# Fourteen unread products ahead of one transposition, and other turning points for three engine loops

## The chip, the cores and the metric

The kernel runs on one core of a Trainium2 chip. The metric is the time of one launch in microseconds, as the device counts it; three runs of the kernel before gave a median of 2035.68 us (2034.31 to 2038.46). The core has five engines that run their own instruction lists and meet only at semaphores: PE (TensorE, products and transpositions), DVE (VectorE), ACT (ScalarE), POOL (GpSimd) and SP (SyncE, which here issues the transfers of x and of the result).

## The reference, cut to what matters

Input x is 32 graphs of 512 nodes with 128 features, adj is one 512 x 512 matrix of zeros and ones that all graphs share. Four layers follow, each `x = layernorm(x + layer(x))`:

```python
x = _layernorm(x + _L0_gnn_ref(x, adj, q, k, v))      # attention, masked with adj
x = _layernorm(x + _L1_gnn_ref(x, adj, Wi, ..., bm))  # gated edges, two small networks
x = _layernorm(x + _L2_gnn_ref(x, adj, weight, bias)) # Chebyshev filter: adj products twice
x = _layernorm(x + _L3_gnn_ref(x, adj, adj, ..., 5))  # five steps of a gated recurrent unit
```

In layer 3 each step computes `m = adj @ h`, gates `r` and `z` from `m` and `h`, a candidate `tanh(...)`, and the new `h`. All is fp32; the large products are taken as two or three passes of high and low parts.

## The kernel before, in words

The 32 graphs are worked on in 8 rounds (0 to 7) of 4 slots (0 to 3); a graph lives in its slot's buffers for a whole round. A round is cut into stages with names: x0, query, scores, mix for layer 0; x1, xh, gates, edges, agg, self, out1 for layer 1; x2, cheb01, cheb23, lap1, lap2 for layer 2; x3 and then m, uh, r, v, rh, t with a step number 0 to 4 for layer 3. "m4.3" is stage m4 of slot 3. `spread` and `norm` 0 to 3 are the layer norms: DVE takes statistics, POOL computes the scale (L396 to L401), ACT applies it (L471).

The order in which an engine takes its stages is fixed ahead of time. `body(engine)` (L119) lays the 64 stages of the 4 slots on one period, shifted per slot and per engine by the numbers in SCHEDULE, and sorts them; what has run past the end of the period is put at its start and marked `behind`, which means that it works for the round before. `run` (L137) writes the stages out three times per engine: the stages of round 0 that are not behind as straight code, then a loop `Fori(1, ROUNDS)` over the whole list, then the stages that are behind once more:

```python
run("tensor", stages, 0, first=True)
with pe.Fori(1, ROUNDS) as r:
    run("tensor", stages, r)
run("tensor", stages, ROUNDS, last=True)
```

So each loop makes seven passes and jumps back six times; the step from the straight code into the loop and the step out of it are no jumps back. Where the list begins is where the loop turns. Before, the turn of all four loops lies at the same part of a round, its end:

- PE: ... m4.3, v4.2, t4.1, uh4.3, rh4.2, r4.3, turn, x0.0, v4.3, t4.2, ...
- ACT: ... m4.2, v4.1, rh4.1, r4.2, turn, m4.3, v4.2, rh4.2, ...
- DVE: ... m4.2, r4.1, last.0, rh4.1, turn, m4.3, r4.2, spread3.0, last.1, rh4.2, ...
- POOL: ... v4.0, m4.2, turn, v4.1, ...

Lines that the rows name: L881 is the transposition helper of PE (x0, x1, x2, x3 and t; `ident` with xin is x0, with X is x1, x2 or x3); L886 to L888 are the three passes of a split product (with U_hi stage uh, with Gw_hi stages r and v, with C_hi stage cheb); L1022 and L1023 are lap1 and lap2; L1050 and L1051 are the eight products of a stage m; L1080 is rh. On DVE L679 writes a low part (gT_lo in stage m), L836 is stage r, L841 and L845 are the two halves of stage rh. On ACT L465 copies a transposition to xT_hi, L471 is a norm, L558 and L559 copy x3's transposition, L563 belongs to stage m. On POOL L425 writes xT_lo in stage m, L430 is stage v.

Around layer 3's start PE's order is lap2.1, lap2.3, x3.0, m0.0, x3.1, uh0.0, m0.1, x3.2, uh0.1, r0.0, m0.2, x3.3, uh0.2, ...; x3.0 waits until ACT has written slot 0's third norm. Before that PE's order around layer 2's start is out1.3, x2.0, x2.1, cheb01.0, x2.2, cheb01.1, x2.3, ...

Of the kernel before, what the change touches and what calls it, by code (L numbers as in the profile page):

```python
# [29 lines left out]
P = 128  # L30
# [83 lines left out]
def elag(engine, n):  # L114

    return SCHEDULE[n][LAGS[engine]] if engine in LAGS else 0.0


def body(engine):  # L119


    period = sum(length for _, length in STAGES) + SLOT_LAG
    at = []
    for s in range(SLOTS):
        time = (s // 2) * PAIR_LAG + (s % 2) * SLOT_LAG
        for n, (name, length) in enumerate(STAGES):
            if name == "lap1" and s % 2 == 0 or name == "spread2" and s % 2 == 1:
                time += SLOT_LAG
            if name not in ("lap1", "lap_lo", "lap2") or s % 2:
                t = time + elag(engine, n)  # L130
                at.append((t % period, s, n, name, int(t // period)))
            time += length
    assert all(behind in (0, 1) for *_, behind in at)
    return [(name, s, behind) for _, s, _, name, behind in sorted(at)]


def run(engine, stages, r, first=False, last=False):  # L137

    for name, s, behind in body(engine):
        if name in stages and not (first and behind) and not (last and not behind):  # L140
            stages[name](s, r - behind)
# [20 lines left out]
TURNS, XTS, GTS, NHS, COPIES, PRODUCTS, VECTORS, POOLS = map(len, (TURNED, XT, GT, NH, COPIED, PRODUCT, VECTOR, POOL))  # L162
DS = 129
NORMS = 4


def build(nc, x, adj, q, k, v, Wi, bi, We, be, Wn, bn, Wm, bm, cheb_w, cheb_b,
# [7 lines left out]
    with ExitStack() as ctx:  # L175
        def sb(name, shape, dt=F32):
            return ctx.enter_context(nc.sbuf_tensor(name, shape, dt))
# [15 lines left out]
        adjT_hi = sb("adjT_hi", [P, TILES, N], F32R)  # L193
# [54 lines left out]
        psA = [ctx.enter_context(nc.psum_tensor(f"psA{s}", [P, N], F32)) for s in range(SLOTS)]  # L248
        psB = [ctx.enter_context(nc.psum_tensor(f"psB{s}", [P, N], F32)) for s in range(SLOTS)]
# [87 lines left out]
        def _(sp):  # L337
# [14 lines left out]
            for r in range(ROUNDS):  # L352
                for s in range(SLOTS):
                    if r + 1 < ROUNDS:
                        sp.wait_ge(residual[s], NORMS * r + 2)
                        sp.dma_start(xin[s][:, :, :], xg[(r + 1) * SLOTS + s]).then_inc(loaded[s], 16)
                for s in range(SLOTS):
                    sp.wait_ge(normed[s], NORMS * (r + 1))
                    sp.dma_start(og[r * SLOTS + s], X[s]).then_inc(stored[s], 16)
# [4 lines left out]
        def _(pool):  # L364
# [28 lines left out]
            def norm(s, r, layer):  # L393

                pool.wait_ge(var_ready[s], NORMS * r + layer + 1)
                nc.gpsimd.tensor_tensor(neg_mean[s][:, :], zero_cols[:, :], mv[s][:, :, 0], ALU.subtract).then_inc(pool_done[s], 1)  # L396
                nc.gpsimd.tensor_tensor(rstd[s][:, :], mv[s][:, :, 1], eps_cols[:, :], ALU.add).then_inc(pool_done[s], 1)
                pool.wait_ge(pool_done[s], POOLS * r + POOL[f"var{layer}"])
                nc.gpsimd.tensor_tensor(rstd[s][:, :], rstd[s][:, :], neg_half[:, :], ALU.pow).then_inc(pool_done[s], 1)  # L399
                pool.wait_ge(pool_done[s], POOLS * r + POOL[f"rstd{layer}"])  # L400
                nc.gpsimd.tensor_tensor(shift[s][:, :], neg_mean[s][:, :], rstd[s][:, :], ALU.mult).then_inc(pool_done[s], 1)  # L401

            def stage_x1(s, r):

                pool.wait_ge(normed[s], NORMS * r + 1)
                pool.wait_ge(turned[s], TURNS * r + TURNED["x1"])
# [20 lines left out]
            def stage_v(s, r, k):  # L427
# [5 lines left out]
                      "cheb23": stage_cheb23}  # L433
            for n in range(NORMS):
                stages[f"spread{n}"] = lambda s, r, n=n: norm(s, r, n)
# [9 lines left out]
        def _(act):  # L445
# [107 lines left out]
            def stage_x3(s, r):  # L553
                i, o = s // 2, s % 2
                act.wait_ge(normed[s], NORMS * r + 3)
                nc.scalar.copy(nh_hi[i][:, :, o, :], X[s]).then_inc(nh_hi_ready[s], 1)
# [320 lines left out]
        def _(pe):  # L877
            def transpose_tiles(dst, src):

                for t in range(TILES):  # L880
                    last = nc.tensor.transpose(dst[:, t * P:(t + 1) * P], src(t), ident[:, :])  # L881
                return last
# [29 lines left out]
            pe.wait_ge(s_flag, 1)  # L912
            inexact = pe.value_load(flag[0:1, 0:1])

            def stage_x0(s, r):
                pe.wait_ge(loaded[s], 16 * r + 16)
                pe.wait_ge(residual[s], NORMS * r + 1)
                transpose_tiles(psA[s], lambda t: xin[s][:, t, :]).then_inc(turned[s], 1)
# [117 lines left out]
                lap(s // 2, psB, exact)  # L1036

            def stage_x3(s, r):
                pe.wait_ge(normed[s], NORMS * r + 3)
                transpose_tiles(psA[s], lambda t: X[s][:, t, :]).then_inc(turned[s], 1)  # L1040

# [44 lines left out]
            def rounds(exact):  # L1086

                stages = {"x0": stage_x0, "query": stage_query, "scores01": stage_scores01, "scores23": stage_scores23,
                          "mix": stage_mix, "x1": stage_x1, "xh": stage_xh, "gates": stage_gates,
                          "edges": stage_edges, "agg": stage_agg, "sums1": stage_sums1, "self": stage_self, "out1": stage_out1, "x2": stage_x2,  # L1090
                          "cheb01": stage_cheb01, "cheb23": stage_cheb23,
                          "lap1": lambda s, r: stage_lap1(s, r, exact), "lap2": lambda s, r: stage_lap2(s, r, exact), "x3": stage_x3}
                for k in range(STEPS):
                    stages[f"m{k}"] = lambda s, r, k=k: stage_m(s, r, k, exact)
                    stages[f"uh{k}"] = lambda s, r, k=k: stage_uh(s, r, k)
                    stages[f"r{k}"] = lambda s, r, k=k: stage_r(s, r, k)
                    stages[f"rh{k}"] = lambda s, r, k=k: stage_rh(s, r, k)
                    stages[f"v{k}"] = lambda s, r, k=k: stage_v(s, r, k)
                    stages[f"t{k}"] = lambda s, r, k=k: stage_t(s, r, k)
# [4 lines that stand above are left out]
# [31 lines left out]
```

## Time and profile before

| what | value |
|---|---|
| median of three runs | 2035.68 us (2034.31 to 2038.46) |
| the profiled execution's own time | 2039.13 us |
| its span, first to last instruction | 2036.8 us |
| mean granted TensorE clock | 0.962 of 2.4 GHz |
| busy: PE, DVE, ACT, POOL | 1856.7, 1472.1, 1354.7, 921.1 us |
| on the chain that ended last: PE, DVE, issue, POOL, ACT | 65%, 13%, 8%, 7%, 7% |

The profile is of one execution. A row of windows gives the stretch in us, its length, the busy time and the instructions of PE, PE's weight loads, DVE, ACT and POOL, and then the granted clock (PEclk, 1.00 is 2.4 GHz), the share of the transfer engines and what they moved in GB/s; a stretch runs from the first product of the one named stage to that of the other. A row of a timeline gives start, duration, engine, line, operation, what is written and read, and in brackets the engine's idle time just before it and what ended it. "issue" is idle time in which the engine waited for nothing that the profile shows.

### The profile page before, as it was taken

Reading aid. Unit: us, or ns where it says so; the run is one execution under the profiler, and the core shown is the slowest. Engines: PE = TensorE matmul, PEld = TensorE weight load, DVE = VectorE, ACT = ScalarE, POOL = GpSimd, SP = SyncE. Lnnn points to the kernel's source line nnn. Section 1 sums busy time; section 2 is a strip of 40 time slices with the busy share of each in tenths; the row PEclk is TensorE's granted clock in tenths of the full one; section 3 lists DMA queues with packets and bytes.
Section 4 is the critical chain, followed back from the end, with each engine's and each line's share of the span. In section 5 each row is a group of like instructions: output and inputs, shape, how many; then the busy total and the mean of one; then the engine's idle time right before and its main releaser. Section 6 shows DMA issues by size and latency. Waiting matters only on the chain.

```text
span 2036.8 us, 27531 instructions
## 1 busy us (share of the span) xinstructions
PE 1856.7 (91%) x9307; PEld 1442.9 (71%) x9307; DVE 1472.1 (72%) x3054; ACT 1354.7 (67%) x2689; POOL 921.1 (45%) x1009
## 2 busy tenths in 40 slices
PE   3899998899998999889998899989999889989997
PEld 2776776777767777577775777757768677676775
DVE  6786688766687667866778667786667866678666
ACT  0766677576766767566775667756768666686666
POOL 2354445445364442634436344363444544345344
PEclk6999999999999999999999999999999999999998
DMA  2000001000010000100000000100001000000000
GB/s 69 22 1 0 1 1 42 1 1 1 7 37 1 1 1 12 32 1 0 1 24 21 1 1 1 43 1 1 1 2 42 0 1 1 2 22 1 0 1 22
DMA packets 13514, 21.32 MB, mean 10 GB/s; under 512 B 2720, under 2 KB 5024, under 8 KB 13216
## 3 DMA queue, kind: packets, MB, share of 16 engines
q1 hardware_dynamic: 10768, 18.68, 2.7%
q8 instruction: 87, 1.43, 0.3%
q10 hardware_dynamic: 2576, 0.53, 0.1%
q14 instruction: 83, 0.68, 0.1%
HBM read 10.82 MB, written 8.39 MB: 9 GB/s over the span
## 4 chain that ended last, share of the span: by engine, by line
PE 65%; DVE 13%; issue 8%; POOL 7%; ACT 7%; DMA 0%; DVEq 0%; SPq 0%; POOLq 0%; ACTq 0%
PE psA L1080 7%; PE psA L1050 7%; PE psA L1051 7%; PE psA L881 5%; PE psB L886 5%; PE psB L888 5%; PE psB L887 5%; PE psA L886 3%; PE psA L888 3%; PE psA L887 3%; PE psB L949 3%; PE psA L949 3%; DVE E L753 2%; ACT X L471 2%; PE psB L1074 2%
## 5 line engine op out<-in xcount | busy, mean ns | idle before, releaser
L430 POOL TENSOR_TENSOR S<-S,H 128x512 f32<-128x512 f32 x160 | 225.1, 1407 | 486.3 <-ACT S L573 486.3
L1050 PE MATMUL psA<-adjT_hi,nh_hi 128*128 128x512 f32 x640 | 275.0, 430 | 11.9 <-ACT H L559 11.6
L471 ACT ACTIVATE X<-X,shift,rstd 128x128 f32<-128x128 f32 x512 | 210.4, 501 | 90.2 <-POOL shift L401 89.2
L1051 PE MATMUL psA<-adjT_hi,nh_lo 128*128 128x512 f32 x640 | 259.8, 406 | 0.0
L425 POOL TENSOR_TENSOR xT_lo<-H,xT_hi 128x512 fp32r<-128x512 f32 x160 | 219.2, 1383 | 71.0 <-ACT xT_hi L581 38.1
L841 DVE SCALAR_TENSOR_TENSOR E<-E 128x512 f32<-128x512 f32 x160 | 181.7, 1135 | 63.3 <-ACT E L577 60.4
L836 DVE SCALAR_TENSOR_TENSOR E<-E,H 128x512 f32<-128x512 f32 x160 | 128.5, 803 | 115.1 <-ACT E L567 114.7
L679 DVE TENSOR_TENSOR gT_lo<-psA,gT_hi 128x512 fp32r<-128x512 f32 x160 | 108.8, 688 | 115.0 <-ACT gT_hi L563 101.1
L396 POOL TENSOR_TENSOR neg_mean<-zero_cols,mv 128x4 f32<-128x4 f32 x128 | 30.8, 240 | 356.1 <-DVE mv L696 355.8
L1080 PE MATMUL psA<-E,u5T 128*128 128x512 f32 x320 | 165.0, 597 | 13.7 <-DVE E L836 13.7
L571 ACT ACTIVATE E<-psB,z_bias 128x512 f32<-128x512 f32 x160 | 110.4, 690 | 81.3 <-PE psB L1074 79.8
L1050 PEld LDWEIGHTS psA<-adjT_hi,nh_hi 128*128 128x128 f32 x640 | 124.5, 195 | 52.1 <-issue 10.8
L567 ACT ACTIVATE E<-psB,r_bias 128x512 f32<-128x512 f32 x160 | 110.1, 688 | 61.7 <-PE psB L888 61.1
L845 DVE SCALAR_TENSOR_TENSOR H<-E,S 128x512 f32<-128x512 f32 x160 | 142.2, 889 | 9.3
L563 ACT CAST gT_hi<-psA 128x512 fp32r<-128x512 f32 x160 | 92.6, 591 | 81.4 <-PE psA L1051 80.8
L1051 PEld LDWEIGHTS psA<-adjT_hi,nh_lo 128*128 128x128 f32 x640 | 125.0, 195 | 29.4 <-issue 3.8
L399 POOL TENSOR_TENSOR rstd<-rstd,neg_half 128x4 f32<-128x4 f32 x128 | 136.4, 1066 | 10.0
L577 ACT ACTIVATE E<-psA,hv_bias 128x512 f32<-128x512 f32 x160 | 109.6, 685 | 26.9 <-PE psA L1080 24.7
L753 DVE SCALAR_TENSOR_TENSOR E<-E,edge_mask 128x512 f32<-128x512 f32 x128 | 124.9, 1034 | 0.0
L976 PE MATMUL psA<-E,U 128*128 128x512 f32 x256 | 115.7, 594 | 0.0
L689 DVE BATCH_NORM_STATS2 stat<-X 128x6 f32<-128x128 f32 x512 | 110.6, 278 | 1.4
L516 ACT ACTIVATE E<-psB,src_bias 128x512 f32<-128x512 f32 x128 | 77.6, 688 | 49.1 <-DVE src_bias L746 24.8
(224 smaller groups left out, 5317.1 us busy)
## 6 DMA issues: line engine op xcount, KB each, us to landing
xin<-in_x SPq DMA_DIRECT2D x32, 256.0 KB, 3.0
out<-X SPq DMA_DIRECT2D x32, 256.0 KB, 2.0
E<-in_adj SPq DMA_DIRECT2D x1, 1024.0 KB, 5.7
E<-in_L_gnn_w_w SPq DMA_DIRECT2D x3, 128.0 KB, 7.2
E<-in_L_gnn_weight SPq DMA_DIRECT2D x1, 192.0 KB, 6.8
E<-in_L_gnn_u_w SPq DMA_DIRECT2D x2, 64.0 KB, 6.9
Wm_sb<-in_L_gnn_Wm ACTq DMA_DIRECT2D x1, 128.0 KB, 7.0
E<-in_L_gnn_q SPq DMA_DIRECT2D x1, 64.0 KB, 5.5
```

Source lines behind the costliest of these rows:

```text
L425: nc.gpsimd.tensor_tensor(xT_lo[s][:, :], H[s][:, :], xT_hi[s][:, :].bitcast(F32), ALU.subtract).then_inc(pool_done[s], 1)
L430: nc.gpsimd.tensor_tensor(kept[s], kept[s], H[s][:, :], ALU.mult).then_inc(pool_done[s], 1)
L471: last = nc.scalar.activation(X[s][:, t, :], X[s][:, t, :], ACT.Identity, scale=rstd[s][:, t:t + 1], bias=shift[s][:, t:t + 1])
L753: nc.vector.scalar_tensor_tensor(out=E[s][:, t, :], in0=E[s][:, t, :], scalar=1.0, in1=edge_mask[:, t, :], op0=ALU.add, op1=ALU.mult).then ...
L841: nc.vector.scalar_tensor_tensor(out=h_new[s], in0=z_gate[s], scalar=1.0, in1=h_new[s], op0=ALU.add, op1=ALU.mult).then_inc(vector_done[s], 1)
L845: nc.vector.scalar_tensor_tensor(out=H[s][:, :], in0=h_new[s], scalar=0.5, in1=kept[s], op0=ALU.mult, op1=ALU.add).then_inc(vector_done[s], 1)
L886: nc.tensor.matmul(dst, w_hi, m_hi, start=start, stop=False)
L887: nc.tensor.matmul(dst, w_hi, m_lo, start=False, stop=False)
L888: return nc.tensor.matmul(dst, w_lo, m_hi, start=False, stop=stop)
L1050: nc.tensor.matmul(psA[s][:, :], hi, adjT_hi[:, m, :], start=(m == 0), stop=False)
L1051: last = nc.tensor.matmul(psA[s][:, :], lo, adjT_hi[:, m, :], start=False, stop=(exact and m == TILES - 1))
L1080: nc.tensor.matmul(psA[s][:, :], U5[:, :], rh[s], start=False, stop=True).then_inc(product[s], 1)
```

## The change

Two edits, both in the order of the work. First, `body` rotates the list of three engines, so that their loops turn at another stage: PE's between x2.1 and cheb01.0, ACT's between lap1.3 and norm2.0, DVE's between m2.3 and r2.0. All stages keep their order on their engine; only which copy of the code a stage comes from changes, and where the jump back lies. POOL's list and SP's are left as they are. Second, PE gets 14 products of 128 x 512 (a tile of the adjacency matrix with a row of it) at the head of stage x3 of slot 0, ahead of that stage's wait. They write psA of slot 0, which the transpositions behind the wait overwrite; nothing reads them. No wait and no transfer is added or taken away.

```diff
+TURN_AT = {"tensor": ("cheb01", 0), "scalar": ("norm2", 0), "vector": ("r2", 0)}
 def body(engine):
...
-    return [(name, s, behind) for _, s, _, name, behind in sorted(at)]
+    order = [(name, s, behind) for _, s, _, name, behind in sorted(at)]
+    if engine in TURN_AT:
+        k = [(name, s) for name, s, _ in order].index(TURN_AT[engine])
+        assert not any(behind for *_, behind in order[k:])
+        order = [(name, s, 1) for name, s, _ in order[k:]] + order[:k]
+    return order
...
+WARM = {"x3": [(0, 0, 0, 14)]}
...
+            def keep_warm(name, s):
+
+                for slot, bank, owner, count in WARM.get(name, ()):
+                    if slot == s:
+                        for _ in range(count):
+                            nc.tensor.matmul((psA, psB)[bank][owner][:, :], adjT_hi[:, 0, 0:P], adjT_hi[:, 0, :],
+                                             start=True, stop=True)
...
             def stage_x3(s, r):
+                keep_warm("x3", s)
                 pe.wait_ge(normed[s], NORMS * r + 3)
                 transpose_tiles(psA[s], lambda t: X[s][:, t, :]).then_inc(turned[s], 1)
```

## Rows read from the trace of the kernel before

**Rows 1.** The page's first part: busy time, share of span, instructions of each engine.

```profile
PE 1856.7 (91%) x9307; PEld 1442.9 (71%) x9307; DVE 1472.1 (72%) x3054; ACT 1354.7 (67%) x2689; POOL 921.1 (45%) x1009
```

**Rows 2.** The waits of PE: idle time in total, times, longest.

```profile
PE psA L881 <- issue: 10.2, 6, 2.3
```

**Rows 3.** Windows (PEclk third last): m4.3 to x2.0, round 0; rounds 1-6 summed.

```profile
277.14:370.43 93.29, 85.74 (x476) 64.89 (x475) 77.74 (x195) 65.56 (x133) 47.24 (x60) 1.00 0.07 24
...
sum 596.19, PE 535.23 PEld 404.83 DVE 471.81 ACT 393.96 POOL 285.75; mean PE 89.21 PEld 67.47 DVE 78.64 ACT 65.66 POOL 47.62
```

**Rows 4.** Timeline of the turn from round 1 to round 2, all engines.

```profile
521.67 0.69 DVE L845 SCALAR_TENSOR_TENSOR H<-E,S 128x512 f32<-128x512 f32 x1
522.44 0.59 ACT L563 CAST gT_hi<-psA 128x512 fp32r<-128x512 f32 x1 [1.93 <-PE psA L1051]
...
524.50 1.27 POOL L430 TENSOR_TENSOR S<-S,H 128x512 f32<-128x512 f32 x1 [3.41 <-ACT S L573]
524.86 0.69 DVE L679 TENSOR_TENSOR gT_lo<-psA,gT_hi 128x512 fp32r<-128x512 f32 x1 [2.50 <-issue]
...
526.37 1.13 PE L1080 MATMUL psA<-E,u5T 128*128 128x512 f32 x2 [2.20 <-DVE E L836]
...
530.07 1.11 PE L881 MATMUL psA<-ident,xin 128*128 128x128 f32 x4 [1.60 <-issue]
```

**Rows 5.** Windows: rh4.2 to the next query.0; round 0, round 1.

```profile
281.54:288.18 6.64, 6.10 (x29) 4.13 (x28) 5.84 (x21) 4.51 (x8) 2.88 (x4) 1.00 0.00 0
526.37:536.47 10.10, 8.50 (x29) 5.93 (x29) 6.42 (x23) 4.21 (x7) 1.27 (x2) 0.66 0.02 4
```

**Rows 6.** Timeline of round 2 around the start of cheb01.0.

```profile
619.53 0.42 PEld L881 LDWEIGHTS psA<-ident,X 128*128 128x128 f32 x4 [0.22 <-ACT X L471]
...
621.90 0.45 PE L886 MATMUL psA<-C_hi,xT_hi 128*128 128x384 f32 x1 [1.71 <-DVE xT_lo L679]
...
623.06 0.60 PE L881 MATMUL psA<-ident,X 128*128 128x128 f32 x4
...
624.66 0.56 ACT L465 CAST xT_hi<-psA 128x512 fp32r<-128x512 f32 x1
```

**Rows 7.** Windows: x2.0 to lap1.1; round 2, then rounds 1 to 6 summed.

```profile
618.95:632.78 13.83, 11.38 (x67) 10.09 (x65) 8.71 (x27) 12.85 (x41) 4.64 (x10) 1.00 0.00 1
...
sum 83.92, PE 70.39 PEld 63.34 DVE 52.24 ACT 77.17 POOL 27.84; mean PE 11.73 PEld 10.56 DVE 8.71 ACT 12.86 POOL 4.64
```

**Rows 8.** Timeline of round 1 around x3.0 and m0.0.

```profile
399.75 0.28 PE L1023 MATMUL psB<-nh_lo,adjT_hi 128*128 128x256 f32 x1
...
401.65 1.65 ACT L471 ACTIVATE X<-X,shift,rstd 128x128 f32<-128x128 f32 x4 [7.41 <-POOL shift L401]
...
403.35 0.66 PE L881 MATMUL psA<-ident,X 128*128 128x128 f32 x4 [3.32 <-ACT X L471]
...
405.77 0.63 PE L1051 MATMUL psA<-adjT_hi,nh_lo 128*128 128x512 f32 x1
...
407.90 0.57 PE L1050 MATMUL psA<-adjT_hi,nh_hi 128*128 128x512 f32 x1
...
409.46 0.50 PE L886 MATMUL psB<-xT_hi,U_hi 128*128 128x512 f32 x1 [0.31 <-POOL xT_lo L425]
...
410.71 0.39 PE L1051 MATMUL psA<-adjT_hi,nh_lo 128*128 128x512 f32 x1
...
412.11 0.39 PE L1051 MATMUL psA<-adjT_hi,nh_lo 128*128 128x512 f32 x1
```

**Rows 9.** Windows: x3.0 to rh0.0; round 1, then all eight rounds summed.

```profile
403.35:423.43 20.08, 18.60 (x78) 14.21 (x79) 10.36 (x29) 15.56 (x32) 8.64 (x13) 0.92 0.00 1
...
sum 165.78, PE 151.76 PEld 115.97 DVE 87.54 ACT 124.45 POOL 67.52; mean PE 18.97 PEld 14.50 DVE 10.94 ACT 15.56 POOL 8.44
```

**Rows 10.** Timeline of round 1 around DVE's stage r2.0.

```profile
465.28 0.69 DVE L679 TENSOR_TENSOR gT_lo<-psA,gT_hi 128x512 fp32r<-128x512 f32 x1 [1.18 <-ACT gT_hi L563]
...
468.89 2.80 DVE L836 SCALAR_TENSOR_TENSOR E<-E,H 128x512 f32<-128x512 f32 x4 [2.92 <-ACT E L567]
```

## The prediction

> **What bounds the kernel now.** I read the page first: PE is busy for 91% of the span [rows 1], so an edit pays where PE stands still or runs at 1.2 GHz, and nowhere else. PE's waits say where: six times it stood before a transposition with nothing to wait for [rows 2]. Six is the number of jumps back that each loop makes in seven passes. The timeline of one such place shows the loops turning one after another: DVE restarts at 524.86, 3.19 us after its last instruction before the jump began at 521.67; PE gets its rh4.2 only then, at 526.37, after 2.20 us idle; and then PE itself turns and restarts with x0.0 at 530.07 [rows 4]. The windows give the price. The stretch from m4.3 to the next round's x2.0 takes 93.29 us from round 0 to round 1, where the code runs straight into the loop, and 596.19 / 6 = 99.37 us in the six rounds with a jump [rows 3]. The stages are the same, so a turn costs 6.08 us. Part of it is the clock: behind the turn PE ran at 0.66 of 2.4 GHz, against 1.00 without a jump [rows 5].
>
> The second weak place is the start of layer 3. PE's last product of lap2.3 starts at 399.75, x3.0's transpositions at 403.35, when ACT's norm has ended [rows 8]. After that pause the products of m0.0 start (407.90 - 405.77) / 5 = 0.426 us apart, those of m0.1 (412.11 - 410.71) / 6 = 0.233 us [rows 8]: 1.2 and 2.4 GHz.
>
> **The change part by part.** The sum is made against the profiled execution, 2039.13 us (span 2036.8); the median of the runs, 2035.68, is 3.45 lower, and the result is moved by as much.
>
> *The turns leave the end of the round.* PE, ACT and DVE then run from m4.3 to x2.0 in each round as they did from round 0 to 1. POOL still turns there, and round 0 does not show that; but in a jump round the 3.41 us in which POOL stood before L430 were ended by ACT, not by its own sequencer [rows 4], so its turn was over by then. What is late next is the dependence of rh4 and t4 among themselves, which round 0's 93.29 contains. Gain: 596.19 - 6 x 93.29 = 36.5 us. Bounds: 0 if something else in those rounds made them longer, 36.5 in full.
>
> *ACT's turn* goes ahead of norm2.0, where ACT is idle for 7.41 us [rows 8]. At the old place ACT was idle for 1.93 us over its turn [rows 4]. Cost 0; if that cover went, up to 1.93 a round, on the chain to x3.0.
>
> *DVE's turn* goes between m2.3's L679, started at 465.28, and r2.0's L836 at 468.89: 3.61 us from start to start [rows 10], where the old turn needed 3.19 [rows 4]. Cost 0, with 0.4 us to spare; without cover at most 3.19 a round.
>
> *PE's turn* goes between x2.1 and cheb01.0. Queued behind it is all of cheb. At the old place PE took 3.70 us from the start of rh4.2, after which only six products ran, to its restart [rows 4]; the mean pause before the restart is 10.2 / 6 = 1.70, not the 1.60 of this row [rows 2], so 3.80. At the new place the last released work starts at 619.53 and cheb01.0 at 621.90, 2.37 later [rows 6]. So cheb01.0 comes 1.43 us late. Some of that is hidden: ACT takes the transposition of x2.2 only at 624.66 [rows 6], being busy for 12.85 of the 13.83 us of this stretch [rows 7]. With the restart at 623.33, six products (621.90 to 623.06) and x2.2 (0.60) end at 625.09, 0.43 late. If the clock falls to 1.2 GHz in the longer pause, these 1.76 us become 1.76 x 0.426 / 0.233 = 3.22 and end 1.89 late. The clock does fall here already in some rounds, with the shorter pause: the sum of 83.92 is 0.94 more than six times round 2's 13.83, which had a clock of 1.00 [rows 7]. I take 1.3 a round, two thirds at the slow clock, part of the way: 6 x 13.83 + 7.8 - 83.92 = +6.9 us. Bounds a round: 0, if the sequencer jumps while products are still queued, and 10.10 - 6.64 = 3.46, all that PE's own turn and its clock cost at the old place [rows 5]; as a sum -0.9 to +19.8.
>
> *The 14 products* do the work of 14 x 0.233 = 3.26 us at 2.4 GHz. They are released at once, behind the product of 399.75, and x3.0 comes 3.60 us after that one's start [rows 8]: they fit, with 0.34 less that one product to spare. Nothing waits for them but the four transpositions. They cost nothing as long as the clock is at 2.4 GHz when they start, as it is through lap2; at 1.2 GHz they would take 14 x 0.426 = 5.96 and make x3.0 2.4 us late.
>
> *What a warm start of layer 3 is worth* is less than it seems. In round 1 m0.0 would end 8 x 0.193 = 1.5 us earlier, but uh0.0 waits for POOL's xT_lo [rows 8], and POOL hangs on norms that PE's clock doesn't touch. Only ACT's copies behind x3.1 come earlier; I take 0.2 us. But round 1, with 20.08 us at a clock of 0.92, is a good one: the eight took 165.78, 20.72 in the mean [rows 9], so others lost more, where already the transpositions ran slowly. With every round at 20.08 - 0.2 = 19.9, the eight take 159.2 instead of 165.78: -6.6 us. Bounds: 0, if POOL holds everything, and 8 x 1.5 more than bringing all to 20.08, -12 - 5.1 = -17.
>
> Sum: -36.5 + 6.9 - 6.6 = -36.2, so 2002.9 for the profiled execution and 2035.68 - 36.2 = 1999.5 us for the median.
>
> **A rule that speaks against it.** DVE stood still for 2.50 us at its turn, and PE for 1.60, with nothing to wait for [rows 4]. The Trainium skill, in "Advanced Engine Details and Errata", Control Flow Timing, gives a branch about 51 ns and a compare with a branch about 108 ns. By that rule alone, six jumps on three engines would be worth some 2 us (an estimate from that page). The trace does not agree. The same page, ISA Cache, says that an engine's instruction cache has only two lines of 256 instructions; no run here shows the cache itself, but a jump far back would then have to fetch its code wherever it lies, and the pauses agree with that.
>
> **The rivals.**
>
> *PE's turn is as dear at cheb01.0 as at x0.0.* For it: x2 already loses its clock in some rounds, and behind the pause lies a chain PE, ACT, DVE. Against: ACT is the busier engine there. With 3.46 a turn: -36.5 + 19.8 - 6.6 = -23.3, 2012.4 us.
>
> *PE's turn is hidden altogether*, since ACT sets the pace: -36.5 - 0.9 - 6.6 = -44.0, 1991.7 us.
>
> *The change doesn't do what it says: the long rounds are not the jumps' doing.* That is what the rule on branches would mean here: the six rounds with 99.37 keep it, for instance since the code must be fetched anyway, and only the start of layer 3 gains: 2029.1 us. Against it: round 0 and the pauses without a reason.
>
> *The products come late.* If the clock has fallen before they start, or the norm comes earlier than now, x3.0 is 2.4 us late eight times: -36.5 + 6.9 + 18.9 = -10.7, 2025.0 us. Against: PE runs without a pause through lap2.
>
> *Slower: three places pay instead of one.* Today the three turns lie within 10 us and overlap. Apart, each could charge in full: PE 3.46, ACT 1.93, DVE 3.19, together 8.58 a round, 51.5 in all. With -36.5, -0.9 and -6.6 that is +7.5: 2043.2 us. It decides from (36.5 + 0.9 + 6.6) / 6 = 7.3 a round. Against it: the idle times of 7.41 and 2.92 us on ACT and DVE [rows 8, 10].
>
> **How the numbers follow.** Forecast 0.60, PE's turn dear 0.19, hidden 0.08, jumps not the cause 0.05, products late 0.04, three places pay 0.04. The forecast's own range is 1992 to 2008. The range reaches from below the hidden case, 1988, past the dear one, 2018, and leaves out the last three cases. About 0.2%, 4 us, is what can be told from no change. The forecast, the dear and the hidden case are all faster, 0.87; of jumps not the cause and of products late 0.03 each are faster and the other 0.03 within; so 0.93 faster, 0.03 same, 0.04 slower.
>
> **What would show it.** The window from m4.3 to x2.0 should be 93.3 us in every round, at clock 1.00; the waits of PE should no longer show six pauses before x0.0, and instead a pause of about 3.1 us before cheb01.0 in rounds 1 to 6. x2.0 to lap1.1 should be about 15.1 in these; from 17 the dear case holds. x3.0 to rh0.0 should be 19.9 in all eight at a clock near 1.00, and x3.0 should still start 3.6 us after lap2.3's last product. DVE's L836 of r2.0 should start 3.6 us after m2.3's L679. The prediction is wrong if the first window stays above 96, or if the three places together take more than 7.3 us a round.

## The result, and the profile after

The changed kernel took 2020.1 us (median of 4 runs, 2019.1 to 2022.1) against 2036.7 for the kernel before, beside which it ran: a ratio of 0.992 [0.9903, 0.9938]. It is faster, by 16.6 us; 36.2 were forecast, and the time lies above the range, 1988 to 2018. The profiled execution took 2019.12 us, its span is 2016.9, 19.9 less than before.

The page of the kernel after: PE's share of the span, and the queue whose packets of 16 KB bring code.

```profile
PE 1857.0 (92%) x9419; PEld 1446.4 (72%) x9419; DVE 1470.6 (73%) x3054; ACT 1354.4 (67%) x2689; POOL 924.1 (46%) x1009
...
q8 instruction: 93, 1.52, 0.3%
```

The waits of PE: idle time in total, times, longest. The six pauses before x0.0 [rows 2] are gone. There are twelve in their place, six on psA and six on psB, 29.5 us where 10.2 stood.

```profile
PE psA L895 <- issue: 18.1, 6, 3.5
...
PE psB L895 <- issue: 11.4, 6, 2.3
```

Windows of m4.3 to the next x2.0 over a jump, round 2 to 3 and the six summed. They are as long as the one without a jump [rows 3]: 93.0 each.

```profile
770.39:863.38 92.99, 85.80 (x475) 64.87 (x474) 77.83 (x195) 65.58 (x133) 47.76 (x60) 1.00 0.07 24
...
sum 558.04, PE 518.19 PEld 393.20 DVE 467.15 ACT 393.47 POOL 286.57; mean PE 86.36 PEld 65.53 DVE 77.86 ACT 65.58 POOL 47.76
```

Windows of x2.0 to lap1.1, the stretch with PE's new turn: rounds 1 and 2, and rounds 1 to 6 summed, as in [rows 7]. The clock is 0.81 where it was 1.00, and a stretch takes 18.24 in the mean. Rounds 0 and 7, which have no jump there, took 13.82 and 13.81.

```profile
370.62:389.55 18.93, 13.02 (x67) 11.90 (x65) 8.71 (x27) 12.99 (x41) 4.63 (x10) 0.82 0.01 3
617.33:635.64 18.31, 13.10 (x66) 12.02 (x65) 8.71 (x27) 12.99 (x41) 4.63 (x10) 0.81 0.01 3
...
sum 109.43, PE 78.97 PEld 72.31 DVE 52.28 ACT 77.92 POOL 27.76; mean PE 13.16 PEld 12.05 DVE 8.71 ACT 12.99 POOL 4.63
```

Windows of x3.0 to rh0.0, round 1 and all eight summed: even, at full clock [rows 9].

```profile
408.20:428.05 19.85, 16.98 (x78) 13.25 (x79) 11.16 (x28) 15.56 (x32) 8.61 (x13) 1.00 0.00 1
...
sum 158.94, PE 136.02 PEld 106.11 DVE 89.48 ACT 124.43 POOL 68.72; mean PE 17.00 PEld 13.26 DVE 11.19 ACT 15.55 POOL 8.59
```

The whole difference of 19.9 is in these stretches, taken over all rounds: m4.3 to x2.0 gave 37.4 (689.48 to 652.08), x3.0 to rh0.0 gave 6.8, the rest 0.2, and x2.0 to lap1.1 took back 24.5 (112.51 to 137.06). So the timeline to read is that of the turn in round 2, where [rows 6] had 621.90 to 623.06 without a gap:

```profile
617.91 0.42 PEld L890 LDWEIGHTS psA<-ident,X 128*128 128x128 f32 x4 [0.22 <-ACT X L480]
...
621.54 0.62 PE L895 MATMUL psA<-C_hi,xT_hi 128*128 128x384 f32 x1 [2.98 <-issue]
...
622.28 0.52 PE L897 MATMUL psA<-C_hi,xT_lo 128*128 128x384 f32 x1
...
624.90 0.48 PE L895 MATMUL psB<-C_hi,xT_hi 128*128 128x384 f32 x1 [2.10 <-issue]
...
625.82 1.05 PE L890 MATMUL psA<-ident,X 128*128 128x128 f32 x4
...
626.91 0.58 ACT L474 CAST xT_hi<-psA 128x512 fp32r<-128x512 f32 x1 [3.78 <-PE psA L890]
```

In these rows L890 is the transposition helper, L895 to L897 are the three passes of a split product and L474 is ACT's copy. PE restarts at 621.54, 3.63 after the start of its last released work (3.80 were forecast); it does three products, and stands still a second time with nothing to wait for. ACT, which was to hide part of the delay, now waits 3.78 for PE. The DMA view of 617 to 631 in 40 slices of 0.35 us, busy tenths and GB/s, shows the code arriving: a 16 KB packet from 618.99, before the restart, the next from 622.57 (slice 16), before the second restart. (The smaller one between is another queue's; nothing waits for the last.)

```profile
DMA  0000010000000001000000000000000000020000
GB/s 0 0 0 0 0 47 0 0 0 0 23 0 0 0 0 47 0 0 0 0 0 0 0 0 0 0 0 0 0 0 0 0 0 0 0 47 0 0 0 0
```

The record of the loop's own branch shows where the first pause comes from. L1119 is PE's loop; the three durations are the shortest, the median and the longest in ns of its seven branches:

```profile
L1119 PEldq COMPARE_BRANCH  x7: 83/3296/3862, 371.3 to 1846.8; - x7
```

The 83 ns are those of the last pass, which doesn't jump back. Each of the six jumps back takes 3.28 us or more.

### The profile page after: what moved, and what is told of

Its sections match the earlier page's. It is cut to its first block, busy times and chain, and to the rows that moved or that the text cites. A ratio compares the mean times of both kernels' runs of the same rounds, so it can differ in the third digit from the quotient of the medians.

```text
span 2016.9 us, 27720 instructions
## 1 busy us (share of the span) xinstructions
PE 1857.0 (92%) x9419; PEld 1446.4 (72%) x9419; DVE 1470.6 (73%) x3054; ACT 1354.4 (67%) x2689; POOL 924.1 (46%) x1009
## 3 DMA queue, kind: packets, MB, share of 16 engines
q8 instruction: 93, 1.52, 0.3%
## 4 chain that ended last, share of the span: by engine, by line
PE 67%; DVE 12%; issue 8%; POOL 7%; ACT 6%; DMA 0%; POOLq 0%; DVEq 0%; ACTq 0%; SPq 0%
PE psA L1068 7%; PE psA L1069 7%; PE psA L1098 7%; PE psB L895 5%; PE psB L896 5%; PE psB L897 5%; PE psA L890 5%; PE psA L895 4%; PE psA L897 3%; PE psA L896 3%; PE psB L966 3%; PE psA L966 3%; DVE E L762 2%; PE psA L993 2%; PE psB L1091 2%
## 5 line engine op out<-in xcount | busy, mean ns | idle before, releaser
L1068 PE MATMUL psA<-adjT_hi,nh_hi 128*128 128x512 f32 x640 | 266.6, 417 | 9.4 <-ACT H L568 9.4
L1069 PE MATMUL psA<-adjT_hi,nh_lo 128*128 128x512 f32 x640 | 253.1, 395 | 0.0
L845 DVE SCALAR_TENSOR_TENSOR E<-E,H 128x512 f32<-128x512 f32 x160 | 126.3, 790 | 115.1 <-ACT E L576 114.7
L688 DVE TENSOR_TENSOR gT_lo<-psA,gT_hi 128x512 fp32r<-128x512 f32 x160 | 108.8, 688 | 94.1 <-ACT gT_hi L572 94.1
L1068 PEld LDWEIGHTS psA<-adjT_hi,nh_hi 128*128 128x128 f32 x640 | 120.4, 188 | 45.2 <-ACT H L568 9.8
L1069 PEld LDWEIGHTS psA<-adjT_hi,nh_lo 128*128 128x128 f32 x640 | 120.5, 188 | 28.1 <-issue 3.8
```

Of the source, the lines that this page charges most:

```text
L1068: nc.tensor.matmul(psA[s][:, :], hi, adjT_hi[:, m, :], start=(m == 0), stop=False)
L1069: last = nc.tensor.matmul(psA[s][:, :], lo, adjT_hi[:, m, :], start=False, stop=(exact and m == TILES - 1))
```

## The experiments

Theory 1: code comes in pieces of 16 KB; the jump's target lies three products before the end of one, and the next piece is asked for only after the restart. The Trainium skill, "Advanced Engine Details and Errata", ISA Cache, gives a line of 16 KB as 256 instructions, and two lines. The packets agree (1.52 MB in 93). Theory 2: the half clock of the first pause does it. Theory 3: the place does it. The three call for moving PE's code without changing it. In what follows "place" is the loop's first instruction by its number in PE's code, modulo 256: 187 in the kernel after, 81 in the one before. The count starts at the program's first instruction and not at the start of a piece; where a piece ends is read off the stops themselves.

**e1 and e2: the code shifted**

```diff
 pe.wait_ge(s_ident, 1)
+for _ in range(56):        # e1, on the kernel after; e2: 72, on the one before
+    nc.tensor.matmul(psA[0][:, 0:1], ident[:, :], ident[:, 0:1], start=True, stop=True)
```

> The changed kernel with 56 unread one-column products (112 instructions) in PE's setup, where PE waits for its first loads: all of PE's code lies 112 instructions further on, nothing else differs. Theory 1 (PE stops twice behind the jump because the jump lands three products before the end of a 16 KB piece of code, and the next piece is fetched only then): the second stop goes, x2.0 to lap1.1 falls from 17.9-18.9 to about 15.5 in rounds 1 to 6, and the time from 2020 to about 2004 us. Theory 2 (the first pause lets the clock fall, and the work at 1.2 GHz costs the rest): one pause is left, the clock falls all the same, x2.0 to lap1.1 stays above 17, time 2012 to 2018. Theory 3 (it is the place: any pause there costs as much, since a chain PE, ACT, DVE stands behind it): no change, 2020.

> The kernel before with 72 such products (144 instructions) in PE's setup, which puts the instruction that its PE loop jumps back to at the same place in a 16 KB piece of code, by counting instructions, as the changed kernel has it: a few instructions before the end. Theory 1: a second stop of about 2 us appears behind x0.0's transpositions in six rounds, m4.3 to the next x2.0 goes from 99.4 to 101.5-102.5, time 2036 to 2049-2055 us. Theories 2 and 3: no change, 2036.

e1: 2025.58 us, 0.9931 [0.9918, 0.9943]. The six stretches fell from 109.43 to 95.55, 15.9 each, as theory 1 had it, but the first x2.0 came at 146.24 instead of 128.34: the added products delayed the start by 17.9, which hides the gain. e2: 2064.22, 1.0115 [1.0100, 1.0130]; its first x2.0 comes 24.6 later than before, which is the whole loss, and the turn itself is unchanged (99.4). It doesn't speak against theory 1: such a product is four instructions and not two (the trace shows plain float32 products in pairs), so the places were 154 and 112. Both were run again as e5 and e6.

**e5: the kernel after, place 83, with no delay of the start**

```diff
+for _ in range(38):
+    nc.tensor.matmul(psA[0][:, 511:512], ident[:, :], ident[:, 0:1], start=True, stop=True)
 pe.wait_ge(s_small, 16 * 15)
```

> The changed kernel with 38 unread one-column products, four instructions each (152), at a place in PE's setup where PE stood 16.6 us for nothing that it could do, so the start of the first round should not move (e1's 56 products cost 17.9 us there). Theory 1 (a second stop, since the jump lands a few instructions before the end of a piece of code): the second stop stays away as in e1, x2.0 to lap1.1 is about 15.7 in rounds 1 to 6 and the time is 24.55 - 11.2 = 13.4 us below the changed kernel's, about 2007, 0.985 of before. Theory 3 (the place): about 2020, 0.992 of before.

2008.20 us, 0.9861 [0.9845, 0.9877]; the first x2.0 at 128.55. Windows of x2.0 to lap1.1, rounds 1 to 3 and the sum:

```profile
370.26:384.43 14.17, 11.03 (x67) 10.07 (x65) 8.72 (x27) 12.99 (x41) 4.65 (x10) 1.00 0.02 4
613.31:629.44 16.13, 12.42 (x67) 11.55 (x65) 8.72 (x27) 13.03 (x41) 4.64 (x10) 0.89 0.01 4
857.17:874.88 17.71, 13.02 (x66) 12.11 (x65) 8.71 (x27) 13.01 (x41) 4.63 (x10) 0.81 0.02 4
...
sum 94.75, PE 73.72 PEld 68.27 DVE 52.29 ACT 78.08 POOL 27.84; mean PE 12.29 PEld 11.38 DVE 8.71 ACT 13.01 POOL 4.64
```

One pause is left in each, and the sum is 14.7 smaller. Theory 3 falls: same place in the program, other place in the code. The rows also price the first pause: 14.17 in the round that kept its clock, 0.34 above 13.83, and 15.79 in the mean, 1.96 above. Round 3 is the longest; there two code packets start 0.30 apart and take 1.8 and 1.7 us.

**e6: the kernel before, place 187**

```diff
+for _ in range(26):
+    nc.tensor.matmul(psA[0][:, 511:512], ident[:, :], ident[:, 0:1], start=True, stop=True)
+nc.tensor.transpose(psA[0][:, 384:512], ident[:, :], ident[:, :])
 pe.wait_ge(s_small, 16 * 15)
```

> The kernel before with 26 such products and one transposition (106 instructions) at the same place of the setup. By counting, its PE loop's first instruction then lies where the changed kernel has it, six to ten instructions before the end of a 16 KB piece of code; e2 had missed that, since a product in plain float32 is four instructions and not two. Theory 1: a second stop of 2.1 to 2.5 us behind x0.0 in six rounds, m4.3 to x2.0 from 99.4 to 101-102.5, 10 to 18 us slower than before, ratio 1.005 to 1.009. Rival: at x0.0 the second stop is hidden by what PE would wait for there anyway; no change, 1.000.

2055.68 us, 1.0088 [1.0074, 1.0101]: the old turn is dearer by 2.8 (613.02 instead of 596.19 for six). The sum of m4.3 to x2.0 over the six, the waits, and the timeline of round 1 to 2:

```profile
sum 613.02, PE 534.12 PEld 400.67 DVE 469.99 ACT 393.52 POOL 283.16; mean PE 89.02 PEld 66.78 DVE 78.33 ACT 65.59 POOL 47.19
```

```profile
PE psA L881 <- issue: 25.4, 12, 2.5
```

```profile
531.12 0.90 PE L881 MATMUL psA<-ident,xin 128*128 128x128 f32 x3 [2.18 <-issue]
534.45 0.48 PE L881 MATMUL psA<-ident,xin 128*128 128x128 f32 x1 [2.43 <-issue]
```

The second stop falls between the third and the fourth transposition of one stage: nothing in the program is there to wait for. It is made by the place alone, in a kernel that never had it.

**e3 and e4: the change taken apart**

```diff
-WARM = {"x3": [(0, 0, 0, 14)]}
+WARM = {}                                                # e3
-TURN_AT = {"tensor": ("cheb01", 0), "scalar": ("norm2", 0), "vector": ("r2", 0)}
+TURN_AT = {"scalar": ("norm2", 0), "vector": ("r2", 0)}  # e4
```

> The changed kernel without the 14 products; the loops turn where the change puts them, at the same place in a piece of code. If the products are what makes x3.0 to rh0.0 even at 19.85: this goes back to a mix of 20.1 and 21.3, 7 us in all, time 2027 us. Rival: the mix came from the jumps at the round's end and the products do nothing: 2020.

> The changed kernel with PE's turn back at x0.0; ACT's and DVE's turns stay moved and the products stay. If PE's own turn costs 3.5 us at x0.0, as the stretch rh4.2 to query.0 showed, and DVE's the rest of 6.1: m4.3 to x2.0 about 96.5, x2.0 to lap1.1 13.8, x3.0 to rh0.0 19.85, time 2012 us, below the changed kernel. Rival (the turns overlap at the round's end, and PE's alone costs the whole 6.1): 2030.

e3: 2031.22, 0.9961 [0.9948, 0.9974]. x3.0 to rh0.0 goes back to 20.1 to 21.3, 166.4 over eight: the products are worth 7.4 there. 2027 us were expected; its twelve runs spread from 2027.17 to 2041.38, wider than any other kernel's, so the 7.4 of the profile is the better measure. e4: 2007.61, 0.9841 [0.9828, 0.9854], better than the whole change: PE's turn back at x0.0 (place 109) costs 570.66 / 6 - 93.01 = 2.1 a round, where 3.5 were expected, while at cheb01.0 it costs 4.4. Against e5's 1.96 at cheb01.0 the old place is hardly dearer: even without the second stop, PE's move brings next to nothing (e5's ratio is 0.9861). The six stretches of m4.3 to x2.0 in e4:

```profile
sum 570.66, PE 520.61 PEld 392.36 DVE 468.75 ACT 395.06 POOL 285.48; mean PE 86.77 PEld 65.39 DVE 78.13 ACT 65.84 POOL 47.58
```

**e7: PE's turn at x3.0, the products ahead of the jump; e12: the same, ACT and DVE turning where they did before**

```diff
+TURN_AT = {"tensor": ("x3", 0), "scalar": ("norm2", 0), "vector": ("r2", 0)}   # e12: "tensor" alone
+WARM = {"lap2": [(3, 0, 0, 14)]}
 def stage_lap2(s, r, exact):
     ...
     lap(s // 2, psB, exact)
+    keep_warm("lap2", s)
 def stage_x3(s, r):
-    keep_warm("x3", s)
```

> The changed kernel with PE's turn at x3.0 instead of cheb01.0, and the 14 products ahead of the jump, at the end of lap2.3, instead of behind it. PE stands 3.6 us before x3.0 anyway. If the sequencer jumps while products are queued, code arrives during them: x2.0 to lap1.1 13.83 in every round, x3.0 at most 0.3 us late, clock kept, time 24.5 us below the changed kernel's, about 1996, ratio 0.980. Rival (the jump waits until the queue is empty): x3.0 comes about 3.3 us later in six rounds, 2016, ratio 0.990.

> e7 with ACT's and DVE's turns back at the round's end; only PE turns elsewhere. e4 showed that PE's turn alone there leaves m4.3 to x2.0 at 95.0, 2.0 above a round without a jump. If the costs there add up: DVE's and ACT's turns are worth the other 4.1, 97.1 in six rounds, time 1996 + 24 = 2020 us. Rival (they overlap, and DVE's 2.2 us at rh4.2 is all): 95.2, 2009 us.

e7: 1995.72 us, 0.9791 [0.9778, 0.9804], the best of all, below both kernels. The timeline of round 1 at the jump, which lies between these two rows: no pause shows. The six stretches of x2.0 to lap1.1 sum up to 83.44, those of m4.3 to x2.0 to 558.02.

```profile
402.03 3.36 PE L931 MATMUL psA<-adjT_hi 128*128 128x512 f32 x14
405.53 0.66 PE L890 MATMUL psA<-ident,X 128*128 128x128 f32 x4
```

The branch of this jump starts at 401.68, and its 16 KB packet at 402.63. The branches are as long as in the kernel after (L1121 is the loop):

```profile
L1121 PEldq COMPARE_BRANCH  x7: 83/3452/3817, 401.7 to 1851.2; - x7
```

So the sequencer jumps, and code is fetched, while products are queued; the jump takes as long as elsewhere, but PE has work meanwhile. e12: 2019.82, 0.9904 [0.9890, 0.9917]. m4.3 to x2.0 takes 97.4 (584.30 for six): ACT's and DVE's turns together cost 4.4 there, PE's alone 2.1 (e4), all three 6.4. The costs at the round's end add up. No run moves ACT's or DVE's turn alone, so how the 4.4 divide is not shown. The six stretches of m4.3 to x2.0 in e12:

```profile
sum 584.30, PE 531.45 PEld 398.84 DVE 471.86 ACT 394.06 POOL 285.02; mean PE 88.57 PEld 66.47 DVE 78.64 ACT 65.68 POOL 47.50
```

**e8 and e11: the clock**

```diff
 def stage_x2(s, r):
     ...
+    keep_warm("x2", s)     # with WARM["x2"] = [(1, 1, 0, 14)]: 14 products into psB[0] behind x2.1
```

> e5 with 14 more unread products between x2.1's transpositions and the jump, so that PE doesn't stand still while code is fetched. It separates the pause from the clock. If the pause's 1.4 us are what the turn costs and the sequencer jumps while products are queued: the clock stays at 2.4 GHz and x2.0 to lap1.1 is about 14.6 to 15.0 against e5's 15.7, 2002 us. If the jump waits until the products are done: cheb01.0 comes 3.3 us later still, x2.0 to lap1.1 about 17.5 to 18, 2017 us.

> e8 with its PE code moved by 76 instructions more, so that the second stop is back while the 14 products ahead of the jump keep the clock. It divides the changed kernel's 4.4 us a turn: x2.0 to lap1.1 is 18.2 with two stops and products absent, 15.7 with one stop (e5), 14.3 with one and the clock kept (e8). If the second stop costs by itself: about 16.3 to 16.8, 2011 us. If it costs mainly through the clock: about 15, 2003 us.

e8 is e5 with this (place 111): 1998.68, 0.9801 [0.9787, 0.9814]. e11 has 57 products in the setup instead of 38 (place 187): 2025.92, 0.9936 [0.9922, 0.9949], of which 5.8 is a later start than e8's. Windows of x2.0 to lap1.1, the sums, e8 and then e11:

```profile
sum 86.39, PE 84.81 PEld 75.49 DVE 52.29 ACT 77.75 POOL 27.76; mean PE 14.13 PEld 12.58 DVE 8.72 ACT 12.96 POOL 4.63
```

```profile
sum 109.91, PE 94.38 PEld 84.31 DVE 52.29 ACT 78.31 POOL 27.81; mean PE 15.73 PEld 14.05 DVE 8.72 ACT 13.05 POOL 4.63
```

e8: 14.40 each; with the clock kept, the first pause costs 0.57 and not 1.96. e11: 18.32, and both of its expectations were too low. Its timeline of round 1 says why:

```profile
379.15 3.46 PE L931 MATMUL psB<-adjT_hi 128*128 128x512 f32 x14
382.84 0.44 PE L895 MATMUL psA<-C_hi,xT_hi 128*128 128x384 f32 x1 [0.23 <-issue]
...
385.93 0.34 PE L895 MATMUL psB<-C_hi,xT_hi 128*128 128x384 f32 x1 [2.29 <-issue]
...
387.08 0.52 PE L896 MATMUL psA<-C_lo,xT_hi 128*128 128x384 f32 x1
```

The products hide the first stop. The second, 2.29 long, comes all the same, and a microsecond into the work behind it the clock falls: a product of 0.34 takes 0.52. The stop and the slow work behind it cost 3.9 a turn. So in these rows the clock is lost once, behind whichever stop PE meets with nothing to do; theory 2 names a part of the price and not the cause.

**e9 and e10: x3.0 without products, and at place 187**

```diff
+WARM = {}                                 # e9, on e7
+for _ in range(28):                       # e10, on e7, and one transposition: 114 instructions
+    nc.tensor.matmul(psA[0][:, 511:512], ident[:, :], ident[:, 0:1], start=True, stop=True)
```

> e7 without the 14 products: PE turns at x3.0 and stands still there while code is fetched. If the products only keep the clock and x3.0's pause of 3.6 us covers the fetch (3.6 to 3.9 from the last released work to the restart in the changed kernel): x3.0 at most 0.3 us late, x3.0 to rh0.0 about 21.3 in six rounds, time 1996 + 9 = 2005 us. Rival (the products also cover a longer fetch): x3.0 over 1 us late, 2011 or more.

> e7 with its PE code moved by 114 instructions in PE's setup, so that the instruction that the loop jumps back to lies six to ten before the end of a 16 KB piece, as in the changed kernel. Theory 1: a second stop of about 2.2 us behind x3.0's transpositions, and m0.0 begins at a lower clock: x3.0 to rh0.0 from 19.85 to 21.3-23 in six rounds, 2005 to 2015 us. Rival (x3.1's norm is awaited there anyway): 1996.

e9: 2003.94, 0.9829 [0.9815, 0.9842]; lap1.1 to x3.0 stays at 18.64, so the fetch fits into the pause of 3.6, and x3.0 to rh0.0 goes to 20.9 (125.30 for six) at a clock of 0.84. e10: 2012.97, 0.9877 [0.9862, 0.9892]; x3.0 to rh0.0 is 23.1 (138.84 for six), and the stop is again behind the third transposition. The sum of the six, and round 1:

```profile
sum 138.84, PE 114.51 PEld 87.51 DVE 61.87 ACT 93.18 POOL 49.51; mean PE 19.09 PEld 14.59 DVE 10.31 ACT 15.53 POOL 8.25
```

```profile
402.61 0.55 PE L890 MATMUL psA<-ident,X 128*128 128x128 f32 x3
405.69 0.27 PE L890 MATMUL psA<-ident,X 128*128 128x128 f32 x1 [2.54 <-issue]
```

All five kernels with place 187 (the one after, e3, e6, e10, e11) stop a second time, at three stages, behind three products or transpositions with their weights; none of the others does (places 45, 73, 81, 83, 109, 111, 112, 154). With the register instructions ahead and, but for e6, the weights of the fourth, the stop comes eight instructions behind the jump's target in all five. Their loops have 2393 to 2449 instructions, so what they share is the target's place and not the place of the jump.

One part of theory 1 is not borne out: that the next piece is asked for only after PE's restart. In all but one of the 84 turns of the 14 kernels (the exception is round 3 of e5) the second packet starts 3.0 to 3.9 us behind the first, at every place. In e9, where x3.0 waits for its norm, it starts before PE does. The DMA view of e9, 398 to 408 in slices of 0.25 us, has the packets from 400.14 (slice 9) and 403.58 (slice 23):

```profile
DMA  0000000040000000000000200000000000000000
GB/s 0 0 0 0 0 0 0 0 98 0 0 0 0 0 0 0 0 0 0 0 0 0 66 0 0 0 0 0 0 0 0 0 0 0 0 0 0 0 0 0
```

```profile
404.67 0.68 PE L890 MATMUL psA<-ident,X 128*128 128x128 f32 x4 [3.32 <-ACT X L480]
```

So the second piece comes at about the same time everywhere. Elsewhere PE has instructions enough of the first piece until then; at place 187 it has eight.

## Why the prediction was wrong, point by point

*The turns leave the end of the round*: right. 36.5 were forecast, the six stretches gave 596.19 - 558.04 = 38.2. POOL's turn, which stays there, costs nothing that shows: 93.01 a round against 93.29.

*ACT's and DVE's turn at 0*: right. For ACT, lap1.1 to x3.0, which ends when its norm is there, takes 18.65 in round 1, against 18.63 before. DVE's L845 of r2.0 starts 3.62 after m2.3's L688, against 3.61 before [rows 10]:

```profile
469.94 0.69 DVE L688 TENSOR_TENSOR gT_lo<-psA,gT_hi 128x512 fp32r<-128x512 f32 x1 [1.18 <-ACT gT_hi L572]
473.56 2.10 DVE L845 SCALAR_TENSOR_TENSOR E<-E,H 128x512 f32<-128x512 f32 x3 [2.92 <-ACT E L576]
```

*The 14 products, and a warm start of layer 3*: right, in size too. x3.0 starts 3.62 behind lap2.3's last product, and the eight stretches gave 6.8 (forecast 6.6). e3 confirms that the products do it.

*PE's turn at cheb01.0*: this is the step that failed. "I take 1.3 a round", with 3.46 as the upper bound; it was 18.24 - 13.83 = 4.4, +25.5 for the six rounds instead of +6.9. The difference of 18.6 is more than the whole miss in the profiled execution, 36.2 - 19.9 = 16.3; the other terms gave a little more than forecast. The restart was forecast rightly, but the step took it for the only stop. A second one follows, since by that layout of the code the target lies eight instructions ahead of the end of a piece; e5 takes it away (-2.4 a turn), e6 and e10 make it elsewhere (+2.8, +3.3). The first stop by itself was also put too low: 1.96 (e5) instead of 1.3. The prediction had worked out 1.89 for a clock that falls, and then took only part of it; in e5 the clock fell in five rounds of six.

The bound of 3.46 was no bound. As the price of PE's own turn at the old place it was too high (e4: 2.1, with the other engines' turns gone); e4 and e12 show that the turns' costs add up, where the prediction let them overlap. As a bound for cheb01.0 it was too low: it was read off the old place, where the target happens to lie 106 instructions earlier in a piece, and it held for that layout only. At place 187 the same turn costs 102.17 - 93.01 = 9.2 together with ACT's and DVE's, instead of 6.4. In the trace of before a second code packet already starts 0.48 behind x0.0's restart at 530.07; what it would do if PE ran out of code before it landed was not asked. The rival "as dear at cheb01.0" thus had the right direction and too low a price; without the second stop, e5's 0.9861 comes to 2007 against the 1999.5 forecast, inside the range.

The Trainium skill's page helped here by half: from ISA Cache's two lines the prediction worked out that a jump back has to fetch its code, which every run agrees with, and not that the fetched line may end a few instructions on. Its 51 ns for a branch in Control Flow Timing are in no trace the price of PE's jump back: the branch alone takes 3.28 us or more above.

What stays open: why the second piece is asked for only 3.0 to 3.9 us behind the first. The runs show that 187 is too late and 154 early enough; places between were not tried.

## What to carry to other kernels

Price a loop's jump back as one fetch of code or two: look in the trace for a second stop with nothing to wait for a few instructions behind the jump's target, which tells that a 16 KB piece ends there. If there is one, shift the code with instructions at a place where the engine is idle; here that was worth 12 us in 2020, and an edit anywhere ahead of the loop can bring it or take it away. Put the jump where the engine waits anyway and queue work ahead of it, as e7 does: the sequencer jumps while the queue is worked off, and in e7 the turn costs nothing. A bound read from one place holds for that place's layout; what sets the price there has to be the same at the other before the bound may be carried over.

## What the runs showed of the hardware that was not expected

- PE's branch takes 3.28 us or more when it jumps back and 0.08 when it doesn't (the kernel after, e7), whether PE stands still meanwhile or not.
- A stop for code of about 2.5 us can stand between two transpositions of one stage (e6, e10).
- Queued products don't hold back the jump: with 14 of them ahead, 3.46 us of work, cheb01.0 restarted 0.23 behind the last (e11), and x3.0 not at all late (e7).
- One-column products in plain float32 are four instructions and cost 0.32 us each at the start (17.9 / 56, e1): shifting code isn't free where the engine isn't idle.
